# Linear attention: score matmuls contracted over 32 rows in row groups, with two masked copies of the keys

## The reference, cut to what matters

```python
q, k, v, u = split(x @ W_qkvu.T)             # 256 features each
q, k = silu(q), silu(k)                      # heads of 16 features
# for each head h, query m, key s <= m:
score[m, s] = dot(q[m, h], k[s, h]) * exp(-slope[h] * (m - s))
o[m, h] = sum_s score[m, s] * v[s, h]
x = layernorm(x + (u * rmsnorm(o)) @ W_out.T)
```

## Time and profile before

| | us |
|---|---|
| median of 3 runs | 1122.48 (1122.47 to 1123.19) |
| the profiled execution | 1117.76 |
| its span | 1116.0 |
| TensorE busy | 941.5 (84%) |
| VectorE busy | 709.5 (64%) |
| ScalarE busy | 412.6 (37%) |
| GpSimd busy | 357.9 (32%) |

### The profile page before, as it was taken

How to read it: one execution, slowest core, us unless ns; L and a number is a source line. 1 busy time by engine, 2 the same in 40 slices (tenths; PEclk the granted TensorE clock), 3 DMA queues, 4 the chain that set the end, 5 groups by cost and what they waited for, 6 DMA issues and landing times.

```text
span 1116.0 us, 16322 instructions
## 1 busy us (share of the span) xinstructions
PE 941.5 (84%) x5120; PEld 706.2 (63%) x5120; DVE 709.5 (64%) x1452; ACT 412.6 (37%) x902; POOL 357.9 (32%) x404
## 2 busy tenths in 40 slices
PE   5638455799999998799989998799989998686997
PEld 4426334574678787664778787664778787323886
DVE  4272569886446689695455799694446799743333
ACT  4101164334423744225224654226224644243221
POOL 2270345321015556030015565030034664000222
PEclk9768768999999999899999999899999999878999
DMA  5200300002013421202014320202022320200342
GB/s 191 101 1 4 136 0 1 1 1 102 1 29 121 133 76 39 82 2 102 1 48 148 95 86 20 83 2 102 1 67 79 96 86 1 81 1 1 103 152 81
DMA packets 21392, 68.46 MB, mean 61 GB/s; under 512 B 2668, under 2 KB 4460, under 8 KB 20148
## 3 DMA queue, kind: packets, MB, share of 16 engines
q1 hardware_dynamic: 21300, 67.32, 18.3%
HBM read 66.27 MB, written 1.05 MB: 60 GB/s over the span
## 4 chain that ended last, share of the span: by engine, by line
PE 43%; issue 31%; DVE 14%; POOL 7%; ACT 4%; DMA 1%; SPq 0%; POOLq 0%; DVEq 0%; ACTq 0%
PE B L755 24%; PE F L755 16%; DVE arena L1395 3%; POOL arena L469 2%; DVE nmx L1459 2%; POOL rs L444 2%; POOL arena L455 1%; ACT arena L551 1%; POOL arena L470 1%; PE B L1027 1%; DVE arena L1402 1%; DMA ctx_t<-in_ctx_t 1%; DVE q_t L1526 1%; ACT q_t L739 1%; DVE xb L1185 1%
## 5 line engine op out<-in xcount | busy, mean ns | idle before, releaser
L755 PE MATMUL B<-k_t,mw 128*128 128x256 f32 x896 | 215.8, 385 | 0.0
L755 PEld LDWEIGHTS B<-k_t,mw 128*128 128x128 f32 x896 | 171.7, 194 | 25.7 <-issue 1.7
L532 POOL TENSOR_TENSOR k_t<-q_t 128x256 f32<-128x256 f32 x112 | 84.2, 753 | 270.9 <-DVE q_t L1531 255.5
L455 POOL TENSOR_TENSOR arena<-du,arena 128x1024 f32<-128x1024 f32 x64 | 150.2, 2356 | 41.2 <-ACT F L662 25.8
L678 ACT ACTIVATE F<-delta,a_neg 128x255 f32<-128x255 f32 x256 | 111.3, 467 | 125.2 <-DVE arena L1395 125.2
L1395 DVE TENSOR_TENSOR_SCAN arena<-F,arena 128x512 f32<-128x512 f32 x128 | 149.2, 1207 | 2.6 <-POOL arena L455 2.6
L755 PE MATMUL F<-arena,ident 128*128 128x256 f32 x512 | 135.8, 413 | 1.5 <-DVE arena L1402 1.5
L1526 DVE SCALAR_TENSOR_TENSOR q_t<-q_t,B 128x256 f32<-128x256 f32 x112 | 47.0, 420 | 117.3 <-ACT q_t L739 117.3
L755 PE MATMUL B<-mw,k_t 128*128 128x256 f32 x448 | 114.5, 380 | 0.6 <-POOL k_t L532 0.6
L755 PEld LDWEIGHTS F<-arena,ident 128*128 128x128 f32 x512 | 102.0, 209 | 16.9 <-DVE arena L1402 1.9
L739 ACT ACTIVATE q_t<-B 128x256 f32<-128x256 f32 x112 | 42.5, 382 | 123.5 <-PE B L755 121.7
(11 more groups left out here) (242 smaller groups left out, 1491.4 us busy)
## 6 DMA issues: line engine op xcount, KB each, us to landing
mw<-in_w_moe SPq DMA_DIRECT2D x112, 384.0 KB, 3.1
room<-in_w_f SPq DMA_DIRECT2D x4, 2672.0 KB, 8.8
room<-in_w_l SPq DMA_DIRECT2D x4, 1280.0 KB, 5.8
w_m<-in_w_m SPq DMA_DIRECT2D x1, 2112.0 KB
x_tok<-in_x_tok SPq DMA_DIRECT2D x4, 256.0 KB, 6.0
x_t<-in_x_t SPq DMA_DIRECT2D x4, 256.0 KB, 6.2
y<-x SPq DMA_DIRECT2D x4, 256.0 KB, 2.2
w_lb<-in_w_lb SPq DMA_DIRECT2D x1, 504.0 KB
```

The source lines that it names most:

```text
L455: g.tensor_tensor(hb[:, n % 4, :, :].rearrange("p d (s t) -> p d s t", s=2), du[:, 2 * dp:2 * dp + 2, :].unsqueeze(2).to_broadcast([P, 2, ...
L532: g.tensor_tensor(hid1[:, m % 3, :], hraw[:, m % 2, :], crs[:, (m // 2) % 2, m % 2, :], ALU.mult)\
L755: return t_.matmul(dst, lhsT, rhs, start=start, stop=stop, skip_group_check=True)
```

## The change

The mask of the keys no longer selects one head of eight. The score matmuls of a head contract only over the 32 partitions that hold it and its neighbour (v // 2 gives the group of 32 partitions), and two masked copies of the keys, for v even and v odd (v % 2), leave the neighbour out. The mask constants have two columns instead of eight, and the constants behind them move by six columns. The two heads of a phase lie in two different groups of 32 partitions, as do any four heads n = 4q to 4q+3, and their scores go to different banks, as they did before. Nothing is moved in the order tables.

```diff
-        headmask = sb("headmask", [P, 8])
+        headmask = sb("headmask", [P, 2])
...
-        kz = arena[:, 0:4096].rearrange("p (f v t) -> p f v t", f=KT, v=8)
+        kz = arena[:, 0:1024].rearrange("p (f v t) -> p f v t", f=KT, v=2)
...
                     for n in (2 * i, 2 * i + 1):
                         f, v = divmod(head(n), 8)
+                        r, c = slice(32 * (v // 2), 32 * (v // 2) + 32), v % 2
...
-                        pe.wait_ge(*df.at(f"kz{v}", b))
+                        pe.wait_ge(*df.at(f"kz{c}", b))
                         bank = F[n % 3]
                         qf = qs.rearrange("p (f t) -> p f t", f=KT)
-                        mm(bank[:, 0:S], kz[:, f, v, 0:P], qf[:, f, :], True, True)
-                        mm(bank[:, S:S + P], kz[:, f, v, P:S], qf[:, f, P:S], True, True)\
+                        mm(bank[:, 0:S], kz[r, f, c, 0:P], qf[r, f, :], True, True)
+                        mm(bank[:, S:S + P], kz[r, f, c, P:S], qf[r, f, P:S], True, True)\
                             .then_inc(pf.step(f"s{n}"), 1)
...
-                    for c in (0, 2, 4, 6, 1, 3, 5, 7):
+                    for c in range(2):
                         v.tensor_scalar(kz[:, :, c, :], ks.rearrange("p (f t) -> p f t", f=KT),
                                         headmask[:, c:c + 1], None, ALU.mult).then_inc(df.step(f"kz{c}"), 1)
...
-        (p // HD0 == np.arange(8)[None, :]).astype(f), (p % 32 == np.arange(32)[None, :]).astype(f)], axis=1)
+        (p // HD0 % 2 == np.arange(2)[None, :]).astype(f), (p % 32 == np.arange(32)[None, :]).astype(f)], axis=1)
```

More of the change, by code:

```diff
@@ L44 @@
 NEG = -1e30
-C_IDENT, C_DIST, C_CAUSAL, C_HEADMASK, C_PARTID, C_END = 0, 128, 384, 640, 648, 680
+C_IDENT, C_DIST, C_CAUSAL, C_HEADMASK, C_PARTID, C_END = 0, 128, 384, 640, 642, 674
 V_WN, V_CW, V_CB, V_BDT, V_D, V_ALOG, V_BK, V_BCS, V_END = 0, 2, 18, 22, 26, 30, 94, 95, 96
@@ L1152, in _ @@
             v.tensor_copy(ident_bf[:, :], arena[:, C_IDENT:C_IDENT + P]).then_inc(init_v, 1)
-            v.tensor_scalar(headmask[:, :], arena[:, C_HEADMASK:C_HEADMASK + 8], 0.25, None, ALU.mult)\
+            v.tensor_scalar(headmask[:, :], arena[:, C_HEADMASK:C_HEADMASK + 2], 0.25, None, ALU.mult)\
                 .then_inc(init_v, 1)
```

## The result

The changed kernel takes 1129.06 us (median of 10 runs, 1125.44 to 1131.96), the kernel before 1122.97 beside it (10 runs, 1117.95 to 1125.42). The ratio is 1.0064, with an interval of 1.0048 to 1.0080: slower by 0.6%, 6.1 us. I had forecast 10.9 us less. In the profiled executions the gap is the same kind of number: 1125.44 us (span 1123.7) against 1117.76 (span 1116.0), 7.7 us.

A forecast was written before the change was run, and what follows sets the result against it. VectorE was taken to bound the loop's attention, a chain of engines the prologue. Three iterations x (2.35 + 0.15) = 7.5, prologue 2.2, clock 1.2: 10.9 us off 1122.48 gives 1111.6; own range 1109 to 1115, wider range 1108.5 to 1119.

The forecast's parts named there:

- The clock in the prologue: Prologue: `wo`, started 2.2 us earlier, would end before the granted clock falls at 42.80; 1.2 us gained.
- 4 rounds x 1.3 us: Rival: the clock falls in the prologue's attention alone, +5 us there, 1118 in all; chance 0.03.
- The row groups: Score matmuls: two heads in two row groups overlap, 0.65 us less a pair, 0.1 to 0.2 per shape change; prologue 2.2.
- The rival without overlap: Scores: a pair keeps its 1.29 us and pays two shape changes; total -2.1 to +1.3, around 1121; chance 0.11.
- the one with dear changes: Rival, scores: groups overlap but each shape change costs 0.4 us; 3.5 us gained, 1119; chance 0.05.
- the reading that only the last instruction of a head would lie beside the next head's first: Scores: by the skill's strict matmul order, the no-overlap rival (chance 0.11) with 0.1 us off each head.
- The six products, 2.35 us: Loop attention: six mask products fewer on VectorE bring 2.35 us in each of three iterations; nothing in the prologue.
- Can they start at 231.39 + 0.9 = 232.3?: Loop: whether VectorE's `q_t` copies can follow two products directly; answered yes, ending at 233.5 instead of 235.85.
- The brackets, 0.15 us an iteration: Loop: of two brackets, 0.87 us, where VectorE waits for a head behind `at4`'s values, 0.15 goes; bounds 0 and 0.87.
- The clock in the loop: Rival: the clock falls in the loop's attention, about +10 us an iteration, about 1149 if all three fall; chance 0.04.
- 19 to 22 us: Loop-clock rival (chance 0.04): TensorE's work in the attention stage, with overlap, falls to this in 28 us.
- The chance of 0.07 for slower: Whole kernel: chance of measuring slower by more than 2.2 us; faster had 0.85, within 0.08.

The follow-up runs named there:

- the second kernel above: Changed kernel with two masked copies kept but scores contracted over all 128 rows (output differs): 1118.57 us beside 1121.26, ratio 0.9972.
- the kernel with the old prologue: Kernel before with the loop changed to two copies and 32 rows, the prologue left at eight copies and 128 rows: 1121.39 us beside 1121.26, ratio 1.0005.

## Why the prediction was wrong

**The clock in the prologue: wrong, and the main miss there.** The step reads "I take 1.2, since nothing I see moves the fall". It moved from 42.80 to 26.50. I had two hints in hand: that TensorE "had idle stretches before it fell, and will have more", and a rival for it, "4 rounds x 1.3 us", with a chance of 0.03. The rounds lengthened by less than that (5.2 us for 4.31, three of them, 2.75 us), but `wo`, which was to win 1.2, lost 2.2. With the first heads' 0.35 gained (0.25 was forecast) that makes +4.6 instead of -3.4, a miss of 8.0 us. What I could not have had from the trace before is that in the prologue even gapless 32-row work doesn't hold the clock.

**The row groups: right.** "Eight score instructions of two heads in about 0.95 us": 0.93, for 1.53. The pitch of a pair with its change of shape is 39.35 - 38.49 = 0.86 us, which is the 0.65 and one change of 0.2, the upper end of what I had. With the clock held, the round is 3.71 for 3.65. The rival without overlap and the one with dear changes fall. So does the reading that only the last instruction of a head would lie beside the next head's first: in the second iteration the second head's first instruction starts at 487.304, 13 ns behind the first head's first, which starts at 487.291, and the first head's next one only at 487.611. The Trainium skill, TensorEngine Tiling (Array Packing), Key Properties, says that a change of mode drains TensorE; a change cost 0.2 us here, within the bounds from the rows.

**The six products, 2.35 us: right in size, wrong in number.** It was 2.38 in the first iteration, 0.20 and 0.19 in the others. The step that failed is "I take 2.35 us in an iteration", and behind it the reading of the earlier trace rows: I showed one iteration and multiplied by three. My own test, "Can they start at 231.39 + 0.9 = 232.3?", asked of the second iteration, has the answer no from a row of the trace before: the transposes start at 477.26, 1.45 us behind the first product at 475.81. What is late next is TensorE, with the transposes and the projections ahead of them, as the second kernel above shows with the old matmuls. That is 4.3 us of the forecast.

**The brackets, 0.15 us an iteration: the right order.** At full clock, with few copies, product to `nmb` in the second iteration is 29.69 for 30.20, of which 0.2 is the products and 0.3 the brackets.

**The clock in the loop: wrong.** It was a rival with 0.04, priced at 10 us for an attention wholly at half clock, "below that VectorE covers it". In the changed kernel it was the last 8 us of one stage: before `nmb` VectorE covered most, and only 1.4 us was lost. The price I had left out stands behind `nmb`: `wo` takes 3.76 us for 1.97, and its result comes 2.7 us later still. The same stretch cost the same in other kernels: between `nmb` and the result of `wo` it is 1.2 us at full clock, and 3.9 both here and in the kernel with the old prologue. So a fall at the end of an attention gives back more than the products had won. How much TensorE had to do was wrong as well: for the "19 to 22 us" of that rival no row was given, and the second attention, whose clock held, has it busy 27.15 of 30.00 us.

The sum by these steps: prologue -3.4 became +4.6; the loop's 7.5 of gain became 2.4 + 0.2 + 0.2 for the products and 0.3 once for the brackets, against 4.1 lost to the clock there. With the load, 0.7 later, and 0.7 more between prologue and loop, that is 7.0 of the 7.7 us; the rest is spread over the stretches between the attentions. The chance of 0.07 for slower was too small chiefly since two rivals on one cause, a clock that I had seen fall, were priced as if rare and separate. One slip changed no forecast: the rival without overlap ends, with 0.2 us lost in each of three iterations and 0.3 more, at +0.9, not +1.3.

## What to carry to other kernels

Before a gain in one iteration of a loop is multiplied, look in each iteration at what the shortened engine meets next. Ask of a change that thins TensorE's work, in rows as much as in time, what follows at the next stretch of half clock, and look beyond the stage: the matmuls right behind it pay, too. And where the clock falls close to a long matmul group, that group's time moves with what happens ahead of it (27.3 to 29.2 us to the result of `wo` in four kernels whose prologue's attention kept its clock), and is not a term to put in a sum.

## What the hardware showed that I had not expected

- Matmuls on 32 rows, two heads side by side, did not keep the granted clock at 1.00 though TensorE was busy 3.40 of 3.40 us; on 128 rows it stayed there with 12.27 of 17.9 us busy, and on 32 rows with some 128-row matmuls between, 15.42 of 19.2.
- Row groups overlap: eight instructions of two heads in 0.93 us. The overlap has a limit in the queue's order. With eight instructions for each head instead of four, TensorE's row in the loop reads

```profile
264.50 2.54 PE L755 MATMUL F<-arena 32*128 32x256 f32 x16
```

  that is 2.54 us for twice what took 0.93. The first head's instructions start at 264.496, 264.816, 265.032, 265.248 and 265.463, and only then, at 265.469, the second head's first. The Trainium skill, TensorE: Matmul & The Clock Gate, Part 3, has matmuls start in strict order. The starts here do not agree: in both kernels the second head's first matmul starts while three of the first head's, which are written ahead of it, are still to come (at 265.469, and at 487.304 in the changed kernel). So TensorE's matmuls do not all start in the order in which they are written, as I had said of every engine. What limits how far ahead one can be I did not test.
- A stretch at half clock at the end of an attention appeared in another iteration when only the prologue was changed (258.60 in the changed kernel, 502.00 with the old prologue). What fixes the iteration is open; each is one profiled execution.
